# A recurrent attention and expert block: linked vector chains overlapped, row norms computed inside the loop, expert outputs scattered to their tokens slot by slot

## What is computed

```python
xn = layernorm(x)                                   # no scale, no bias
# attention, 16 heads of 8; q = k = v = p
p = xn @ Wv.T + bv
s = softmax(p p^T / sqrt(8)) p  @ Wo.T + bo         # per batch and head
# experts, 8 of them, the 2 best per token
z = layernorm(xn) * ln_g + ln_b
probs = softmax(z @ rW + rb); w = the two largest, normalised
mixed = sum over the two: w_e * (gelu(z @ W1[e] + b1[e]) @ W2[e] + b2[e])
g = silu(xn + mixed)
out = x + s * g
```

## Time and profile before

| | |
|---|---|
| median of 3 runs (lowest to highest) | 638.71 us (637.45 to 641.12) |
| the profiled execution's own time | 637.87 us |
| its span, first to last instruction | 636.1 us |
| busy: PE, ACT, DVE, POOL | 571.2 (90%), 542.5 (85%), 244.5 (38%), 152.1 (24%) |
| DMA | 81.39 MB, 104059 packets |

### The profile page before, as it was taken

How to read it: one execution, slowest core, us unless ns; L and a number is a source line. 1 busy time by engine, 2 the same in 40 slices (tenths; PEclk the granted TensorE clock), 3 DMA queues, 4 the chain that set the end, 5 groups by cost and what they waited for, 6 DMA issues and landing times.

```text
span 636.1 us, 11439 instructions
## 1 busy us (share of the span) xinstructions
PE 571.2 (90%) x3994; PEld 234.0 (37%) x3994; DVE 244.5 (38%) x709; ACT 542.5 (85%) x591; POOL 152.1 (24%) x170
## 2 busy tenths in 40 slices
PE   3666279999999999799999999999979999999995
PEld 2544033233434344333434444444433344433221
DVE  5673474772333333123222232223213663212463
ACT  5354146999999999999999999999998999999994
POOL 2334206777720000000000000000353700005760
PEclk9979555999999999879999999999986999999998
DMA  5117595767555554326454544453333756422230
GB/s 162 30 42 195 191 298 175 258 214 177 142 139 141 128 133 104 84 77 138 109 129 111 132 116 108 106 142 94 97 80 103 199 152 176 124 70 73 59 84 25
DMA packets 104059, 81.39 MB, mean 128 GB/s; under 512 B 51403, under 2 KB 95966, under 8 KB 103390
## 3 DMA queue, kind: packets, MB, share of 16 engines
q1 hardware_dynamic: 99902, 72.23, 42.7%
q0 software_dynamic: 4096, 8.40, 4.4%
HBM read 58.03 MB, written 28.32 MB: 136 GB/s over the span
## 4 chain that ended last, share of the span: by engine, by line
PE 66%; ACT 12%; DVE 8%; issue 5%; SPq 5%; DMA 2%; POOL 0%; ACTq 0%; DVEq 0%
PE bank_v L1238 32%; PE pair L1179 15%; ACT exps L712 9%; PE bank_f L1284 8%; PE bank_f L1275 7%; ACT pre L686 1%; PE bank_f L1255 1%; PE bank_f L1262 1%; DMA p_dram<-o_ring 1%; SPq L493 1%; DVE newton L736 1%; DVE rows_in_sb L746 1%; SPq L494 1%; DVE o_turned L992 1%; SPq L516 1%
## 5 line engine op out<-in xcount | busy, mean ns | idle before, releaser
L712 ACT ACTIVATE exps<-pair 128x1024 f32<-128x1024 f32 x512 | 488.1, 1052 | 47.6 <-PE pair L1179 29.8
L1238 PE MATMUL bank_v<-exps,v_tok 128*32 128x512 f32 x2048 | 282.4, 624 | 2.4 <-DVE o_turned L992 1.7
L1179 PE MATMUL pair<-q_ring,k_ring 26*128 26x512 f32 x1024 | 155.1, 510 | 11.9 <-ACT exps L712 9.9
L624 POOL DMA_INDIRECT rows_in_sb<-o_dram,dest_i x64 | 61.8, 966 | 375.5 <-DMA o_dram<-o_ring 342.8
L1179 PEld LDWEIGHTS pair<-q_ring,k_ring 26*128 26x128 f32 x1024 | 61.8, 186 | 107.2 <-ACT exps L712 66.1
L614 POOL DMA_INDIRECT z_dram<-pre,dest_i x64 | 63.6, 994 | 45.7 <-DVE dest_i L947 26.5
L1284 PEld LDWEIGHTS bank_f<-w_ring,pre 128*128 128x128 f32 x320 | 45.7, 206 | 71.4 <-issue 45.8
L1284 PE MATMUL bank_f<-w_ring,pre 128*128 128x128 f32 x320 | 61.9, 320 | 9.6 <-ACT pre L686 5.2
L1027 DVE TENSOR_TENSOR pre<-bank_f,w_ring 128x256 f32<-128x256 f32 x80 | 33.9, 423 | 94.5 <-PE bank_f L1275 94.5
L1275 PEld LDWEIGHTS bank_f<-zT,w_ring 128*128 128x128 f32 x320 | 41.7, 190 | 68.4 <-DVE pre L1027 46.8
L1238 PEld LDWEIGHTS bank_v<-exps,v_tok 128*32 128x32 f32 x2048 | 41.3, 110 | 69.3 <-ACT exps L712 38.3
(11 more groups left out here) (139 smaller groups left out, 281.7 us busy)
## 6 DMA issues: line engine op xcount, KB each, us to landing
w_ring<-w_dram SPq DMA_DIRECT2D x80, 192.0 KB
w_ring<-w_dram SPq DMA_DIRECT2D x80, 129.0 KB
q_ring<-p_dram SPq DMA_DIRECT2D x56, 104.0 KB
k_ring<-p_dram SPq DMA_DIRECT2D x56, 96.0 KB
z_dram<-s_tok SPq DMA_DIRECT2D x4, 1280.0 KB, 8.8
z_ring<-z_dram SPq DMA_DIRECT2D x80, 64.0 KB
o_dram<-o_ring SPq DMA_DIRECT2D x20, 256.0 KB, 2.4
p_dram<-z_ring SPq DMA_DIRECT2D x8, 256.0 KB, 2.9
```

Of the source, the lines that this page charges most:

```text
L624: pool.indirect_dma_start(rows_in_sb[:, (h * HT + i) % GATHER_RING, c, :], None, o_dram[h][:, :], bass.IndirectOffsetOnAxis(dest_i[:, h, c ...
L712: nc.scalar.activation(exps[:, g % ES, 2 * half:2 * half + 2, :], pair[(2 * g + half) % 3][:, :, :], ACT.Exp, scale=SCALE).then_inc(exp_do ...
L1179: ins = nc.tensor.matmul(pair[h % 3][:, j % 2, :], k_ring[32 * j:32 * j + KROWS, n % 2, kt * P:(kt + 1) * P], q_ring[32 * j:32 * j + KROWS ...
L1238: ins = nc.tensor.matmul(bank_v[32 * j:32 * j + 32, :], v_tok[:, (n // HG) * KT + kt, first:first + 32], exps[:, g % ES, j, :], start=(kt ...
```

## The change

- **Norms of the prologue.** Groups of 8, 8 and 16 tiles. Statistics of later tiles are issued beside the linked instructions of a chain (`link(..., beside)`), m2 beside the third link of the first norm. The first load of x goes ahead of Wv; four instead of six warming matmuls stand behind the branch. `norm2` is one chain for all tiles, between two `keep_p`.
- **Row norms.** Only blocks 0 and 1 (`EARLY`) keep theirs in the prologue. Blocks 2 to 7 become uses of `bank_f` at steps 13 to 18 (`norm`); DVE reads each into a buffer of two, which for block g waits until the store of block g - 2 has landed (`m_kept`), and SP stores it a step later (`store_norms`), to a row that it reads from `m_row_i`. ACT's wait for all stores at steps 2 and 3 goes; unit 4 waits for them instead.
- **Steps.** Ranking, counting, assigning, weighing and scaling of z stand some steps later. The biases are eight uses of two columns at 4 to 6 and 8 to 12; the counts stand at 7 and 24; `zero_z(1)` at 12 instead of 16; the scaled W1 at 17 instead of 13; `keep_w2` at 33 instead of 24; the first z loads at 34. The expert uses begin at 37 (first placed at 38) with a spacing of 1.19 instead of 36 and 1.12: the last one stands at 230 instead of 225.
- **Way back of the rows.** `assign` also computes where a choice's entry stands in a table by slot and row (`place_i`, five more linked instructions for each choice). POOL scatters the numbers of the tokens' places into it (`place`, 32 indirect DMAs per half, 4 bytes a row, at 54 to 75 and 77 to 98); SP loads the table back (`load_places`, 77 and 100). POOL scatters each slot's rows of `o_ring` right after its `down` (`store_o`, 80 indirect DMAs of 128 rows), to `o_dram`, now in token order; rows without a token go to spare rows behind. SP then loads two tiles with both rows in one dense DMA (`load_rows`, 16 in all), and `combine` takes a tile every 3/4 step, from 184 and 237. The last `gate` of the loop stands at 251 instead of 257, the last but one `finish_y` at 252 instead of 258.

The core of the diff (the parts left out are steps, names and the Gram sums):

```diff
-NORMS = ((0, 4), (4, 4), (8, 8), (16, 8), (24, 8))
-WARM = (4, 6)
+NORMS = ((0, 8), (8, 8), (16, 16))
+WARM = (4, 4)
+EARLY = NB // B
...
-SCATTER_AT = (6, 22)
-MOE_AT = 36
-MOE_STEP = 1.12
-GATHER_LAG = 3
+NORM_AT = 12
+ZERO_AT = 12
+SCALE_W1_AT = (13, 14, 15, 16)
+SCATTER_AT = (11, 31)
+MOE_AT = 37
+MOE_STEP = 1.19
+LOAD_LAG = 5
+PLACE_AT = (54, 77)
...
+    for g in range(EARLY, NB):
+        place(("norm", g), NORM_AT + g - EARLY)
...
-                if g == 2:
+                if g == EARLY:
+                    for e in range(EARLY):
+                        sp.wait_ge(n2_copied, e + 1)
+                        sp.dma_start(p_dram[:, M_ROW, e * BLK:(e + 1) * BLK], m_blk[:, e, :]).then_inc(m_kept[0], 16)
...
-                sp.wait_ge(n2_copied, g + 1)
-                sp.dma_start(p_dram[:, M_ROW, tokens], m_blk[:, g, :]).then_inc(m_kept[g // 4], 16)
...
+            def store_norms(g):
+                sp.wait_ge(bank_f_read, written("norm", g))
+                sp.dma_start(p_dram[:, bass.ds(m_row, 1), g * BLK:(g + 1) * BLK], m_blk[:, g % 2:g % 2 + 1, :]).then_inc(m_kept[1 + g % 2], 16)
...
-            def store_o(q):
-                h, k = divmod(q, QUADS)
-                sp.wait_ge(bank_f_read, written("down", q, 3))
-                sp.dma_start(o_dram[h][k * 4 * P:(k + 1) * 4 * P, :].rearrange("(a p) d -> p a d", p=P), o_ring[:, q % 2, :, :]
-                             ).then_inc(o_stored[q % 2], 16)
+            def load_places(h):
+                sp.wait_ge(placed[h], HT * 2 * 16)
+                sp.dma_start(slot_place[:, h, :], place_dram[h][:, :].rearrange("(p s) o -> p (s o)", p=P)).then_inc(slot_place_in[h], 16)
+            def load_rows(h, i):
+                t = h * HT + i
+                if i == 0:
+                    for c in range(2):
+                        sp.wait_ge(o_stored[c], (h + 1) * QUADS // 2 * 64)
+                if t >= ROW_RING:
+                    sp.wait_ge(combined, t - ROW_RING + LOAD_TILES)
+                sp.dma_start(rows_in_sb[:, t % ROW_RING:t % ROW_RING + LOAD_TILES, :, :],
+                             o_dram[t * P * 2:(t + LOAD_TILES) * P * 2, :].rearrange("(t p c) d -> p t c d", p=P, c=2)
+                             ).then_inc(rows_loaded[t // LOAD_TILES % ROW_LOADS], 16)
...
+                for e in range(EARLY, NB):
+                    if g == AT["norm", e] + 1:
+                        store_norms(e)
+                if g == ZERO_AT:
+                    zero_z(1)
...
-            def gather(h, i):
...
+            def place(h, i):
+                if i == 0:
+                    pool.wait_ge(places_zeroed, 32)
                 for c in range(2):
+                    pool.indirect_dma_start(place_dram[h][:, :], bass.IndirectOffsetOnAxis(place_i[:, h, c, i:i + 1].bitcast(U32), 0),
+                                            token_place[:, h * HT + i, c:c + 1], None).then_inc(placed[h], 16)
+            def store_o(q, i):
+                h, k = divmod(q, QUADS)
+                pool.wait_ge(bank_f_read, written("down", q, i))
+                if k == 0 and i == 0:
+                    pool.wait_ge(slot_place_in[h], 16)
+                pool.indirect_dma_start(o_dram[:, :], bass.IndirectOffsetOnAxis(slot_place[:, h, 4 * k + i:4 * k + i + 1].bitcast(U32), 0),
+                                        o_ring[:, q % 2, i, :], None).then_inc(o_stored[q % 2], 16)
...
-                if 2 <= g < 4:
-                    act.wait_ge(m_kept[g - 2], NB // 2 * 16)
...
+                elif what == "norm":
+                    g = arg[0]
+                    if g < EARLY + 2:
+                        dve.wait_ge(m_kept[0], 16 * EARLY)
+                    else:
+                        dve.wait_ge(m_kept[1 + g % 2], (g - EARLY) // 2 * 16)
+                    ins = nc.vector.tensor_scalar(m_blk[:, g % 2, :].bitcast(F32R), bank_f[0:H, :], -1.0, None, ALU.mult)
...
+                elif what == "norm":
+                    pe.wait_ge(sq_ready, arg[0] + 1)
+                    ins = nc.tensor.matmul(bank_f[0:H, :], head_sel[:, :], sqT[:, arg[0], :], start=True, stop=True)
```

More of the change, by code:

```diff
@@ new lines, in inverse_root, with statistics @@
+                    link(nc.vector.tensor_tensor(some, some, variance, ALU.mult), beside)
+                    link(nc.vector.scalar_tensor_tensor(out=scale, in0=some, scalar=1.5, in1=scale, op0=ALU.add, op1=ALU.mult), beside)
+            tiles = iter(range(NT))
+            def statistics():
+                t = next(tiles, None)
+                if t is None:
+                    return None
+                for chunk, (start, _) in enumerate(X_CHUNKS):
+                    if t == start:
+                        dve.wait_ge(x_in[chunk], 16)
+                return nc.vector.bn_stats(stats[:, t, :], x_tok[:, t, :])
@@ L753, in norm1 @@
+            def norm1(c, first, count, beside=None):
+                some = slice(first, first + count)
+                for t in range(first, first + count):
+                    ins = nc.vector.bn_aggr(mv[:, t, :], stats[:, t, :])
+                link(ins)
+                link(nc.vector.tensor_scalar(veps[:, some], mv[:, some, 1], EPS, None, ALU.add), beside)
+                inverse_root(veps[:, some], rstd[:, some], beside)
                 nc.vector.scalar_tensor_tensor(out=shift[:, some], in0=mv[:, some, 0], scalar=-1.0, in1=rstd[:, some],
```

244 lines of the change are left out of this document (133 added, 111 removed).

## The result

The changed kernel takes **630.48 us** (median of 4 runs, 628.34 to 632.46) against 638.42 of the kernel before beside it (4 runs, 637.45 to 641.12): a ratio of **0.9867 [0.9828, 0.9906]**, 8 us gained where 15 were forecast. The profiled execution is the slowest of the four (own time 632.46, span 630.7). Medians and ratios in this document leave out executions that stand more than 1.5% above the fastest of the same kernel, which happened in experiments 9 and 11 alone.

A forecast was written before the change was run, and what follows sets the result against it. ACT's exponentials set the settled loop's pace, PE steps with expert work; the loop's start lost time to the expert-count wait and low clock. 13.4 + 1.0 + 0.9 = 15.3 off 637.87, plus 0.84: 623 us, range 598 to 637.

The forecast's parts named there:

- the stall at step 3: PE's waits for the expert count, 8.46 and 1.54 us before; forecast to return at step 16, some 20 us long.
- Prologue: Before the loop: m2 at 13.5, first unit's loads at 39.8, first exponential at 49.5 instead of 57.83, 8.3 us gained.
- SP and its queue: SP's DMA order: zeroing near 68, copies at 79.9, first loop norm store landing at 102 behind them (96.7 to 103.9).
- The steps before the stall: Loop up to step 16: PE at norm 5's bank use at about 81, then a gap of 15 to 25 us.
- Exponential 34: ACT at step 17, once the norm store has landed: starts near 104.2 instead of 122.5, 18.3 us ahead.
- Behind the stall: Up to step 20: cold steps cost 2.2 us, norms on PE 1.2, norm 7's wait 1.5, leaving 13.4 ahead.
- Expert stage: Expert uses spread over 193 steps instead of 189: a gain of 1.0 us, between 0 and 1.7.
- Way back: POOL's scatters replacing gathers, dense loads on SP: counted as 0 us.
- Tail: After the last projection only the last pair of tiles is left: a gain of 0.9 us, between 0 and 1.5.
- No stall: Rival: the norm store lands like a lone one, step 16 is 37.9 us ahead, SP late at step 37; 607, chance 0.24.
- Nothing gained ahead of the loop: Rival: unit 0's loads start no earlier than 48.12, 13.4 shrinks to about 3; 634 to 638 us, chance 0.11.
- POOL the bound: Rival: POOL's in-order scatters delay o_ring's reuse at step 105, making the kernel slower; 644 us at 2.6 each, chance 0.09.

The follow-up runs named there:

- experiments 9 and 11: Changed kernel with six row buffers and one dummy product per score half: 620.24 us; that with z loads earlier, old way back and old spread: 616.00 us.
- experiments 1 to 3: Changed kernel with, in turn, a row buffer for each loop norm (619.90 us), norm stores on ACT's queue (621.73), second zeroing at step 21 (625.72).
- experiment 3: Changed kernel with the second zeroing moved from step 12 to 21, behind the norm stores: 625.72 us.
- experiment 1: Changed kernel with a row buffer for each of the six loop norms, so none waits for a store to land: 619.90 us.
- old spread kernel: Changed kernel with the expert stage spread as before (from step 36, spacing 1.12) and the new way back: 628.65 us.

## Why the prediction was right, and where its sizes were off

The sign and the mechanism were right: the stall at step 3 went, and came back at step 16 as DVE's wait in norm 4's read, behind the zeroing in SP's queue. Both are shown, by the waits of the changed kernel and by experiments 1 to 3. The size was 15.3 us in the sum and 5.4 in the profiled span (8 by the medians). Point by point:

- *Prologue*: first exponential 49.5 forecast, 52.73 measured, so 5.1 of 8.3. m2 came sooner than taken (11.8 instead of 13.5), but what stood behind it took longer: the first head load is at 41.07 where I had 39.8, and from there to the first exponential went 11.7 us instead of 9.7. It did not reach the sum, as the next three points show.
- *SP and its queue*: zeroing at 68 (68.19), copies at 79.9 (80.07), the row's landing at 102 (104.94). These issues were right to 0.2 us; the landing was 2.9 late, just beyond the upper end of 103.9. That SP waits for nothing between the zeroing and the norm stores was wrong: its issues end at 83.47, and norm 2's row, which DVE read at 91.27, went out at 92.17. The landing was the queue's all the same, since with the zeroing gone from in front of it (experiment 3) norm 4's read did not wait.
- *The steps before the stall*: I had PE at norm 5's use at about 81 and a gap of 15 to 25 us. PE was there at 96.55 and sat 9.13: steps 4 to 14 took 3.1 us each instead of 1.86, with two waits for DVE's bias reads (3.3 us in all) and part of them at 1.2 GHz. The sum does not depend on it, because the landing lets the loop go on; it is why the kernel without the wait (experiment 1) stands 24 us ahead there and not 38.
- *Exponential 34*: forecast 104.2 and 18.3 ahead; measured 107.03 and 15.3 ahead. All of the difference is that landing.
- *Behind the stall*: forecast 2.2 for cold steps, 1.2 for norms and 1.5 for norm 7's wait, 13.4 ahead at step 20. Measured 9.7 there and 8.1 from step 22 on. **Norm 7's wait is the term that was mis-sized**: 4.39 on DVE, 4.5 us of lead. Norm 5's read ended at 106.98, but SP issued its store at 108.86, behind W1's two issues, and it landed 7.0 us later. The row for that was there, 7.0 for a small store behind this megabyte; I had reckoned with the megabyte's own 5.8. The rest, up to step 22, is 2.7, where cold steps and norms had 3.4.
- *Expert stage*: forecast a gain of 1.0 from the wider spread; measured a loss of 4.0 from step 24 to 255, of which 1.5 go at the first gelu with the longer time at 1.2 GHz, and 1.4 behind step 196, where work that stood behind the loop now stands in it and the tail gets it back. **The spread gained nothing**: from step 24 to 82 the lead stays within 1 us. Why the rest goes (some 1 us) I did not settle.
- *Way back*: forecast 0; the whole says 0, within some 2 us (0.9888 without it, 0.9857 with it at the same spread).
- *Tail*: forecast 0.9, measured 5.4 - 4.1 = 1.3.

The misses add up: 3.0 (landing), 2.3 (behind the stall) and 5.0 (expert stage) less 0.4 (tail) are the 9.9 between 15.3 and 5.4. They are those of one execution, the slowest of the four. The old spread kernel has the same work up to step 27 and stood 11.0 ahead at step 24 instead of 8.0, so some 3 us of them differ from one execution to the next.

The rivals. *No stall* was false for this kernel. Experiment 1, which takes the stall out, bears out its second half, SP late for z, at 6.5 us where I had said 9, but not its first: the lead is 24 and not 37.9, for the steps before the stall. (Its 607 also leaves out the 0.84 that the forecast adds: 608.) *Nothing gained ahead of the loop* was false: the first head load stands at 41.07, 39.8 forecast. (13.4 less 8 is 5.4 and not about 3, so this rival began at 631.) *POOL the bound* was false: 0.97 us each, and 238.0 us of idle time; the writes of 4 bytes a row, for which I cited a rule, cost POOL no more than rows of 512 bytes.

## What to carry to other kernels

A small store that frees a buffer belongs on a queue with nothing big in it, if the engine that issues it can wait for its data, or gets a buffer of its own; before moving work behind a wait, list what its engine's DMA queue will hold at that moment, in bytes. When a stall is removed, look at once for the next late thing on the same in-order engine: here each cure (rows, then z's place in SP's list) showed the next one behind it (z, then the scatters). And work added to keep PE busy is a gamble: with one dummy a half, six executions took 615 to 621 us and six 638 to 646.
